# Experts weighted with finished shares and scattered onto the residual in the output tensor

## The reference, cut to what matters

```python
probs = jax.nn.softmax(logits, axis=-1)
_, idx = jax.lax.top_k(logits.T, top_k)          # 16 experts x 128 tokens
xe = xn[idx]
h = jax.nn.gelu(einsum(xe, fc1_weight) + fc1_bias, approximate=False)
y = einsum(h, fc2_weight) + fc2_bias
gates = jnp.take_along_axis(probs.T, idx, axis=1)
output = zeros.at[flat_idx].add((y * gates[:, :, None]).reshape(-1, d))
gate_sums = zeros1.at[flat_idx].add(gates.reshape(-1, 1))
output = jnp.where(gate_sums > 0, output / gate_sums, output)
x = x + jnp.tanh(g_ffn[1]) * output
```

## Time and profile before

| | us |
|---|---|
| median of 3 runs | 2018.47 (2015.37 to 2020.93) |
| the profiled execution, its own time | 2009.03 |
| its span, first to last instruction | 2007.2 |
| TensorE busy in the span | 1791.8 (89%) |
| VectorE busy | 1293.6 (64%) |
| DMA: moved | 101.72 MB, mean 51 GB/s |

### The profile page before, as it was taken

The page is one execution under the profiler, slowest core; times in us unless marked ns, Lnnn a source line. Parts: engine busy times, 40 slices in busy tenths (PEclk is TensorE's granted clock), DMA queues, the critical chain, the costliest instruction groups (busy, mean ns, idle before and its releaser), DMA issues. The chain is left out here.

```text
span 2007.2 us, 32393 instructions
## 1 busy us (share of the span) xinstructions
PE 1791.8 (89%) x11428; PEld 1164.9 (58%) x11428; DVE 1293.6 (64%) x2785; ACT 1037.6 (52%) x2198; POOL 685.6 (34%) x1002
## 2 busy tenths in 40 slices
PE   6989999999899797998899989999998998871895
PEld 3445555555567465765576765557776554550794
DVE  5579999999623485333799953269997444968112
ACT  3489999999521265221677741157775112640221
POOL 0023333333333344242555541135555112550422
PEclk9999999999999899999999999999999998985897
DMA  3451111110000200020000002010000000046695
GB/s 120 139 157 44 43 44 43 43 44 2 1 1 1 63 1 1 1 64 28 18 7 6 5 6 66 0 45 4 5 6 6 20 1 16 1 149 149 209 309 157
DMA packets 104896, 101.72 MB, mean 51 GB/s; under 512 B 34896, under 2 KB 88480, under 8 KB 104608
## 3 DMA queue, kind: packets, MB, share of 16 engines
q1 hardware_dynamic: 101664, 95.31, 15.7%
q0 software_dynamic: 3072, 4.34, 1.1%
HBM read 80.60 MB, written 16.92 MB: 49 GB/s over the span
## 5 line engine op out<-in xcount | busy, mean ns | idle before, releaser
L612 DVE TENSOR_REDUCE negmax<-sps 128x1 f32<-128x1024 f32 x256 | 308.7, 1216 | 17.6 <-PE sps L534 13.0
L656 ACT ACTIVATE prob<-sps,negmax 128x1024 f32<-128x1024 f32 x256 | 285.7, 1117 | 23.6 <-DVE negmax L612 19.1
L1532 POOL TENSOR_TENSOR la_pr<-la_pr,la_ri 128x512 f32<-128x512 f32 x128 | 158.6, 1269 | 153.3 <-DVE la_ri L1596 153.3
L702 POOL TENSOR_TENSOR probT<-probT,after 128x128 f32<-128x128 f32 x256 | 117.5, 459 | 237.4 <-DVE probT L620 211.6
L1786 ACT ACTIVATE la_pr<-la_pr,la_nx 128x256 f32<-128x256 f32 x256 | 126.4, 495 | 100.6 <-DVE la_nx L1637 100.6
L534 PE MATMUL sps<-ks,qs 128*128 128x512 f16 x512 | 170.1, 384 | 7.8 <-PEq L42 3.1
L1971 PE MATMUL la_bs<-lf_zT,lfw 128*128 128x512 f32 x352 | 153.0, 594 | 0.0
L550 PE MATMUL tps<-ident,prob 128*128 128x128 f32 x704 | 125.3, 282 | 22.5 <-DVE probT L620 20.2
L550 PEld LDWEIGHTS tps<-ident,prob 128*128 128x128 f32 x704 | 79.6, 140 | 89.2 <-issue 44.1
L1542 POOL TENSOR_TENSOR la_qs<-la_qn,ores 128x256 f32<-128x256 f32 x128 | 96.3, 783 | 76.8 <-DVE la_qn L1653 76.8
L1971 PEld LDWEIGHTS la_bs<-lf_zT,lfw 128*128 128x128 f32 x352 | 66.4, 190 | 82.5 <-issue 82.3
(11 more groups left out here) (379 smaller groups left out, 3871.8 us busy)
## 6 DMA issues: line engine op xcount, KB each, us to landing
w1e<-in_fc_T SPq DMA_DIRECT2D x16, 1024.0 KB, 6.0
w2e<-in_fc_T SPq DMA_DIRECT2D x16, 1024.0 KB, 9.0
qs<-q_parts SPq DMA_DIRECT2D x128, 64.0 KB, 1.9
ks<-k_parts SPq DMA_DIRECT2D x128, 64.0 KB, 1.9
q_parts<-parts SPq DMA_DIRECT2D x8, 512.0 KB, 3.7
k_parts<-parts SPq DMA_DIRECT2D x8, 512.0 KB, 3.6
lfw<-in_L_ffn_w SPq DMA_DIRECT2D x6, 640.0 KB
ores<-in_L_ffn_wqkv SPq DMA_DIRECT2D x2, 1536.0 KB, 6.4
```

The costliest lines, as they stand in the source:

```text
L612: dve.tensor_reduce(negmax[:, n % 4:n % 4 + 1], slots[n % NS][:], X, ALU.max, negate=True).then_inc(s.max_done, 1)
L656: act.activation(prob[:, n % 3, :], slots[n % NS][:], ACT.Exp, bias=negmax[:, n % 4:n % 4 + 1], accum_out=rowsum[:, tile % 2, n % QUAD:n % ...
L702: pool.tensor_tensor(blk, blk, after[:], ALU.mult).then_inc(s.masked, 1)
L1532: ins = pool.tensor_tensor(prob[:, h:h + 2, :], prob[:, h:h + 2, :], rinv[:, h:h + 2].unsqueeze(2).to_broadcast([P, 2, 2 * P]), ALU.mult)
```

## The change

The weights that a token receives are added up before any expert is weighted, not taken from the scattered column.

- The selection keeps `logits` (round 0 writes its result to a second tile, `work`). In the expert block, `choose` on VectorE compares `logits` with `least` (and, where logits are equal to it, the place with that of the last one taken), so that a 0/1 tile `chosen` says which token each expert takes. TensorE turns it in two transposes (`turn_chosen`, behind fc1(1), into a half of `by[1]`). `coefficients` multiplies by the probabilities, adds over the experts, inverts, multiplies by the gate and by the probabilities: `scaled` is each token's 16 finished shares. SyncE writes them to `share_rows` in HBM (2048 rows of 64 bytes).
- For each expert GpSimd gathers the 128 rows of shares by the same `idxT` into `mine`, and weigh multiplies by its column.
- `token_rows` has only the 256 channels, and each group is stored once its rows are normalised. `mixed` and its zeros are gone; SyncE writes the residual xres (2 MB) to the output in the router block, and the scatters add to the output itself, 256 values a row. The reload, the coefficients, the products and the stores behind the last scatter are gone.
- The router block now issues the gathers of experts 0 and 1. The expert block issues those of experts 2 to 6, waits for the shares to have landed, gathers the shares of experts 0 to 2, and then, in each round ahead of the scatter, shares(e+3) and tokens(e+7).

The diff, cut: moved allocations, the semaphore names and the new tiles are left out.

```diff
-        AROW = D + 1
         assert CAP == P
-        token_rows = nc.dram_tensor("token_rows", (TOK, ROW), F32).ap()
-        mixed = nc.dram_tensor("mixed", (TOK, AROW), F32).ap()
+        token_rows = nc.dram_tensor("token_rows", (TOK, D), F32).ap()
+        share_rows = nc.dram_tensor("share_rows", (TOK, E), F32).ap()
...
+        out_rows = out.rearrange("b t c -> (b t) c")
...
-                    sp.wait_ge(s.zeroed, 1)
-                    sp.dma_start(mixed.rearrange("(t p) c -> p t c", p=P),
-                                 zero[:].unsqueeze(1).to_broadcast([P, NT, AROW])).then_inc(s.mixed_zero, 16)
                     for r in range(RING):
...
                     for g in range(G):
-                        sp.wait_ge(s.probs_done, g + 1)
+                        sp.wait_ge(s.row_done, g * J + J)
                         sp.dma_start(token_rows.rearrange("(t p) c -> p t c", p=P)[:, g * J:(g + 1) * J, :],
-                                     row[:, g, :, :]).then_inc(s.rows_out, 16)
+                                     row[:, g, :, 0:D]).then_inc(s.rows_out, 16)
+                    sp.wait_ge(s.x_done, G * J)
+                    sp.dma_start(out.rearrange("b (t p) c -> p (b t) c", p=P), xres[:]).then_inc(s.base_out, 16)
                     with nc.allow_non_contiguous_dma(reason="biases by channel"):
                         sp.dma_start(b1e[:], io["L1_ffn_fc1_bias"].rearrange("e (k p) -> p e k", p=P)).then_inc(s.next_in, 16)
                     sp.dma_start(b2e[:].rearrange("p e c -> p (e c)"),
                                  io["L1_ffn_fc2_bias"].rearrange("e c -> (e c)").unsqueeze(0).to_broadcast([P, E * D])).then_inc(s.next_in, 16)
                     sp.wait_ge(s.rows_out, 16 * G)
-                    sp.wait_ge(s.mixed_zero, 16)
+                    sp.wait_ge(s.base_out, 16)
                     sp.wait_ge(s.next_in, 32 + 32 * RING)
...
-                    pool.memset(zero[:], 0.0).then_inc(s.zeroed, 1)
...
-                    pool.indirect_dma_start(out=xe[:, 0, :], out_offset=None, in_=token_rows,
-                                            in_offset=bass.IndirectOffsetOnAxis(ap=idxT[:, 0:1], axis=0)).then_inc(x_in[0], 16)
+                    for e in range(2):
+                        pool.indirect_dma_start(out=xe[:, e, :], out_offset=None, in_=token_rows,
+                                                in_offset=bass.IndirectOffsetOnAxis(ap=idxT[:, e:e + 1], axis=0)).then_inc(x_in[e], 16)
...
+                        held = logits if r == 0 else work
                         if r > 0:
                             dve.wait_ge(s.removed, r)
-                        dve.max(best[:, e8], logits[:]).then_inc(s.best_done, 1)
+                        dve.max(best[:, e8], held[:]).then_inc(s.best_done, 1)
...
-                            dve.match_replace(logits[:], best[:, e8], logits[:], -3.4028235e38).then_inc(s.removed, 1)
+                            dve.match_replace(work[:], best[:, e8], held[:], -3.4028235e38).then_inc(s.removed, 1)
...
+            p_in = [nc.alloc_semaphore(f"e_p_in{i}") for i in range(E)]
...
+                    sp.wait_ge(s.scaled_done, 1)
+                    sp.dma_start(share_rows.rearrange("(t p) e -> p t e", p=P), scaled[:]).then_inc(s.shares_out, 16)
                     for e in range(RING, E):
                         r = e % RING
...
                     sp.wait_ge(s.added, 16 * E)
-                    for g in range(G):
-                        sp.dma_start(acc[:, g * J:(g + 1) * J, :],
-                                     mixed.rearrange("(t p) c -> p t c", p=P)[:, g * J:(g + 1) * J, :]).then_inc(mixed_in[g], 16)
-                    for g in range(G):
-                        sp.wait_ge(s.x_done, (g + 1) * (J - 1))
-                        sp.wait_ge(s.last_done, g + 1)
-                        sp.dma_start(out.rearrange("b (t p) c -> p (b t) c", p=P)[:, g * J:(g + 1) * J, :],
-                                     fin[:, g * J:(g + 1) * J, :]).then_inc(s.x_out, 16)
-                    sp.wait_ge(s.x_out, 16 * G)
...
+                    def tokens(e):
                         pool.indirect_dma_start(out=xe[:, e, :], out_offset=None, in_=token_rows,
                                                 in_offset=bass.IndirectOffsetOnAxis(ap=idxT[:, e:e + 1], axis=0)).then_inc(x_in[e], 16)
+
+                    def shares(e):
+                        pool.indirect_dma_start(out=mine[:, e, :], out_offset=None, in_=share_rows,
+                                                in_offset=bass.IndirectOffsetOnAxis(ap=idxT[:, e:e + 1], axis=0)).then_inc(p_in[e], 16)
+
+                    for e in range(2, 7):
+                        tokens(e)
+                    pool.wait_ge(s.shares_out, 16)
+                    for e in range(3):
+                        shares(e)
                     for e in range(E):
+                        if e + 3 < E:
+                            shares(e + 3)
+                        if e + 7 < E:
+                            tokens(e + 7)
                         pool.wait_ge(s.weighted, e + 1)
-
                         if e > 0:
                             pool.wait_ge(s.added, e * 16)
-                        pool.indirect_dma_start(out=mixed, out_offset=bass.IndirectOffsetOnAxis(ap=idxT[:, e:e + 1], axis=0),
+                        pool.indirect_dma_start(out=out_rows, out_offset=bass.IndirectOffsetOnAxis(ap=idxT[:, e:e + 1], axis=0),
                                                 in_=gated[:, e % 2, :], in_offset=None, compute_op=ALU.add).then_inc(s.added, 16)
-                    pool.wait_ge(s.added, 16 * E)
-                    for g in range(G):
-                        t = g * J + J - 1
-                        pool.wait_ge(s.last_scaled, g + 1)
-                        pool.tensor_tensor(fin[:, t, :], fin[:, t, :], xres[:, t, :], ALU.add).then_inc(s.last_done, 1)
 
...
-                        dve.wait_ge(x_in[e], 16)
-                        dve.tensor_copy(gated[:, e % 2, D:AROW], xe[:, e, D + e:D + e + 1]).then_inc(s.gate_done, 1)
                         dve.wait_ge(s.fc2_done, e + 1)
-                        dve.tensor_tensor(gated[:, e % 2, 0:D], by[e % 2][:], b2e[:, e, :], ALU.add).then_inc(s.biased, 1)
+                        dve.tensor_tensor(gated[:, e % 2, :], by[e % 2][:], b2e[:, e, :], ALU.add).then_inc(s.biased, 1)
                         dve.wait_ge(s.biased, e + 1)
-                        dve.tensor_scalar(gated[:, e % 2, 0:D], gated[:, e % 2, 0:D], xe[:, e, D + e:D + e + 1], None,
+                        dve.wait_ge(p_in[e], 16)
+                        dve.tensor_scalar(gated[:, e % 2, :], gated[:, e % 2, :], mine[:, e, e:e + 1], None,
                                           ALU.mult).then_inc(s.weighted, 1)
 
-                    def coefficients(g):
-                        t = slice(g * J, (g + 1) * J)
-                        dve.wait_ge(mixed_in[g], 16)
-                        dve.scalar_tensor_tensor(out=total[:, t], in0=acc[:, t, D], scalar=0.0, in1=acc[:, t, D],
-                                                 op0=ALU.is_le, op1=ALU.add).then_inc(s.total_done, 1)
-                        dve.wait_ge(s.total_done, g + 1)
-                        dve.reciprocal(coef[:, t], total[:, t]).then_inc(s.inverse_done, 1)
-                        dve.wait_ge(s.inverse_done, g + 1)
-                        dve.tensor_scalar(coef[:, t], coef[:, t], gate[:, 3:4], None, ALU.mult).then_inc(s.coef_done, 1)
-
-                    def result(g):
-                        dve.wait_ge(s.coef_done, g + 1)
-                        for t in range(g * J, g * J + J - 1):
-                            dve.scalar_tensor_tensor(out=fin[:, t, :], in0=acc[:, t, 0:D], scalar=coef[:, t:t + 1],
-                                                     in1=xres[:, t, :], op0=ALU.mult, op1=ALU.add).then_inc(s.x_done, 1)
+                    def choose():
+                        slot = pick[:, 2 * P:3 * P]
+                        dve.scalar_tensor_tensor(out=last[:], in0=place[:], scalar=1.0, in1=used[:],
+                                                 op0=ALU.add, op1=ALU.mult).then_inc(s.last_done, 1)
+                        dve.tensor_tensor(equal[:], over[:, 1, :], over[:, 0, :], ALU.subtract).then_inc(s.equal_done, 1)
+                        dve.wait_ge(s.last_done, 1)
+                        dve.wait_ge(s.equal_done, 1)
+                        dve.tensor_tensor(last[:], last[:], equal[:], ALU.mult).then_inc(s.tie_done, 1)
+                        dve.wait_ge(s.tie_done, 1)
+                        dve.tensor_reduce(bound[:, 0:1], last[:], X, ALU.max).then_inc(s.bound_done, 1)
+                        dve.wait_ge(s.bound_done, 1)
+                        dve.tensor_scalar(bound[:, 1:2], bound[:, 0:1], -float(CAP), None, ALU.add).then_inc(s.bound_done, 1)
+                        dve.wait_ge(s.bound_done, 2)
+                        for q in range(PAIR):
```

(46 more changed lines are left out.)

46 lines of the change are left out of this document (28 added, 18 removed).

## The result

| | before | changed |
|---|---|---|
| median of the runs, us | 2019.70 (2015.37 to 2021.78, 4 runs) | 1997.58 (1995.37 to 1999.81, 4 runs) |
| profiled execution, its own time | 2009.03 | 1995.37 |
| its span | 2007.2 | 1993.6 |

The changed kernel is faster: ratio 0.9893 [0.9877, 0.9909], 22.1 us between the medians. Two differences stand side by side: between the two profiled executions 13.7 us, which is the sum that was predicted; between the medians 22.1. The rest of this text is about the 8 us between them.

The account below looks back on a forecast made before the run. Two chains of nearly equal length, TensorE (7.25 us an expert) and the scatters (7.06 a round), over nearly full DMA engines, then a 16.3 us tail. -16.3 + 2.5 + 0.1 = -13.7 took 2018.5 to 2004.8 us, range 1999 to 2012.

Parts of the forecast that it names:

- the sum: All terms together: -16.3 + 2.5 + 0.1 for clearing 16 more semaphores = -13.7 us; chance of 11 to 16 us, 55%.
- The tail: Behind the last scatter's landing: reload, divisions, products and stores go, 2006.3 - 1990.0 = 16.3 us off, hidden by nothing.
- The line of scatters: Expert loop: scatter 0 starts 5.8 us later, rounds of 7.6 and 7.3, then 4.6; last landing 2.5 us later, at 1992.5.
- The store of the shares: Ahead of the first weighting: writing 2048 pieces of 64 B to HBM takes 4.0 us, bounds 1.9 and 8.
- TensorE: Expert block: fc1 1.4 us sooner, transposes +0.22, 2.2 idle before expert 3's fc1; end +1.0 us, bounds -1.3 and +5.
- Router block: Before the expert block: 2 MB of residual replaces 2 MB of zeros, landing within some 20 us of cover, at no cost.
- B: Rival: cheap start, scatter rounds stay at 7.06 us; 17.6 us gained, 2001; chance 20%.
- D: Rival, slower: each scatter waits in its queue for the two gathers issued before it, rounds of 9.3 us, 2029; chance 6%.

Follow-up runs that it names:

- b_split: Kernel before with gathers 1 to 6 in a row and the others one in each round: 2010.53 us, ratio 0.9966 to before.
- a_front_2: a_front run once more, on another chip: 2003.14 us, ratio 0.9931 to the kernel before.
- a_front: Changed kernel with eleven token gathers in a row in the expert block instead of five: 1995.98 us, ratio 0.9930 to the kernel before.
- b_no_tail: Kernel before without reload, division and store behind the last scatter, output only the residual: 1993.78 us, ratio 0.9921 to before.
- a_no_shares: Changed kernel without its sums, its store and gathers of shares, weighting by the raw gate: 1993.89 us, ratio 0.9916 to the kernel before.
- b_pause: Kernel before with GpSimd stopping behind gather 3 until expert 0's fc1 is done, then twelve gathers in a row: ratios 1.0002 and 1.0000 to before.
- b_thin: Kernel before with the gathers of experts 3 to 15 fetching 16 values a row instead of 272: 2018.92 us, ratio 1.0004 to before.
- b_rows256: Kernel before with rows of 256 values instead of 257, sums of gates left out: 2016.07 us, ratio 0.9997 to before.
- b_gather1: Kernel before with gather 1 issued in the router block: 2015.83 us, ratio 0.9994 to before.
- a_again: Changed kernel, unchanged, timed again on chip 2: 1993.79 us, ratio 0.9877 to the kernel before.
- b_row10: Kernel before with gathers 1 to 10 in a row and 11 to 15 one in each round: ratios 0.9992 and 0.9995 to before.

## Why the prediction was wrong

**The step that failed** is the one that set the base: "The median of the runs is 2018.47, 9.4 above that execution: 2018.5 - 13.7 = 2004.8." It carried those 9.4 us over as if they lay outside the two blocks that change. By all that the later runs show, some 7 of them lay inside: on chips where the kernel before takes 2016 the profiles of its variants show TensorE, ScalarE and VectorE held back around expert 0's fc2 while GpSimd issues gathers without a stop, and the change cuts that row from 15 gathers behind the barrier to 5. The edit that did it, gathers 7 to 15 moved into the rounds, had no term of its own in the sum; its only price was inside the rounds. The loss is shown by taking it away (`b_split`, 5.8 to 6.9 us by the times, 7.3 to 7.6 by the traces) and by bringing it back (`a_front_2`: 6.3 us more than `a_front` by the traces, 7.2 by the medians of two chips). That it was also the loss of the first measurement is not shown outright, since the timed executions of before have no trace there. Two things speak for it: the like differences (22.1 us there; 22.3 and 21.2 on chips 2 and 6), and ScalarE's 6.50 us in the trace of the changed kernel, the mark of such chips. The remaining 1 us or so lies within what the start of the blocks adds to one execution or another.

**The tail, -16.3**: right, 15.7 by the medians of `b_no_tail` and 15.1 by its trace. In the terms of the traces: what follows the last landing was 2007.2 - 1990.0 = 17.2 and is 3.0, so -14.2. I had given it 1.0. `b_no_tail` and `a_no_shares`, which also end on a scatter, have 2.0 and 2.1; `a_no_shares` clears the same 16 further semaphores, so the clearing is not what makes 3.0 of it. What fills these two or three us no trace names.

**The line of scatters, +2.5**: 1990.6 instead of 1990.0, +0.6. From scatter 0 to the last landing I forecast 1992.5 - 1887.5 = 105.0 us; it took 105.0, at 7.55 a round and 4.6 for the last four. What was mis-sized is the start: scatter 0 at 1885.57 instead of 1887.5, because the shares landed in 3.0 us, not 4.0, GpSimd woke in 0.2, not 0.7, and they were ready at 1875.97 instead of 1876.5. The two small errors, -1.9 and +2.0, cancel by luck: span forecast 1993.5, measured 1993.6.

**The store of the shares**: 2048 pieces of 64 B in 3.0 us, the side of the small copies. The Trainium skill ("DMA: Bandwidth & Descriptors", Anatomy of one DMA — SWDGE (gpsimd) path) gives an estimate of 2.3 by its fit, which is for DMAs issued from GpSimd, while SyncE issued this one. The same page of the Trainium skill (Specifications) says that below 512 B the DMA does a read-modify-write; nothing near the upper bound of 8 shows here.

**TensorE**: fc1 1.13 us earlier (1.46 counted from gather 0; forecast 1.4), idle 0.9 ahead of expert 3 in place of 2.2. Its last fc2 ends at 1983.35, and as said the scatters decide.

**Router block**: cost nothing, as said. SyncE waited 7.5 us for the last bias, before 6.9, and gather 0 starts within the spread of its other executions.

**Rivals**: B (17.6 us, rounds at 7.06) had the direction and the wrong place: the rounds are 7.55. Its 7.06 was also misread: 71.5 us over 13 waits is a mean with the short ones of the end in it, and scatters 0 to 11 of the kernel before lie 7.26 us apart. D, the scatter queued behind its gathers, did not come; with six gathers moved out of the rounds (`a_front`) they are just as long. None of the rivals was a gain in the row of gathers.

## What to carry to other kernels

When the profiled execution is far from the median of the timed runs, the gap is a term like the others: ask whether it can lie in the block that changes, and widen the range on that side. When indirect DMAs are regrouped, cost the length of the uninterrupted row on GpSimd too, not only their place in the queue: spreading them over the rounds, each as far ahead as it must be, cost nothing here and was worth about 7 us on the chips that showed the loss. Count the times of two executions from a common event just ahead of the change, so that what differs before it drops out. And a chain that starts 6 us late but has slack against another may end 1 us late (`b_pause`): price a shifted start by where the two chains meet.

## What the runs showed of the hardware

On three of the six chips used (before at 2016.1, 2016.35 and 2016.1) the kernel before takes 7 us more than on the other three (2009.5, 2009.1, 2009.0). On two of them, by the traces, a row of 11 to 15 indirect gathers issued by GpSimd at a pitch of 1.25 us goes with pieces and gaps of 0.2 to 1.7 us on TensorE, and with a standstill of ScalarE and VectorE, until 2.3 to 2.75 us after the row's end; on the chips of 2009 the same row goes without it. It does not go with the bytes of the gathers (`b_thin`: 8 KB instead of 136), and not with instructions being loaded (no packet on their queues from 1870 to 1890). TensorE's granted clock falls to 0.50 in the gaps, and the next fc1 of the kernel before takes 4.7 to 5.3 us instead of 3.73 (`b_rows256`, `b_gather1`).

Rows of 5 and 6 leave TensorE and VectorE free (`a_again`, `b_split`). ScalarE's first gelu is 1.4 us late beside the row of 5 on chips 2, 3 and 6 (6.42 us behind its table load, 5.00 on chip 1), and not late in `b_split` (8.58, before 8.57), where its input is ready only 2 us after the row of 6 has ended.

The Trainium skill ("Trainium Architecture — The Big Picture", What this means for kernel authors) names one pair of engines that contend in on-chip memory, VectorE and GpSimd; since TensorE and ScalarE stand too, that pair alone does not explain these rows. What the engines lack while they stand, at which length between 6 and 11 it reaches TensorE, whether it needs the moment at which expert 0's fc2 starts, and why only some chips have it, stays open. The two kernels made to tell length from moment, `b_pause` and `b_row10`, ran only on chips without the loss.
